# A fused attention and mixture-of-experts block on one core: another order of the opening's loads and products, and another order of products in the expert stage

## The chip, the cores and the metric

The kernel runs on one core of one Trainium2 chip. A core has five engines with queues of their own: TensorE (PE, with its weight loads shown apart as PEld), VectorE (DVE), ScalarE (ACT), GpSimd (POOL) and SyncE (SP). They meet through semaphores. SP, ACT and POOL also issue DMA transfers. The metric is the device time of one execution in microseconds, here the median of the runs. Matmul is meant by "product" below.

## The reference, cut to what matters

x is (2, 256, 32, 32): two images b, 256 channels, 1024 positions ("tokens").

```
h   = group_norm(x, 32 groups) * norm_w + norm_b
q,k,v = conv1x1(h) with wq, wk, wv (+ bq, bk, bv)
x   = x + conv1x1(softmax(q^T k / 16) applied to v, wp) + bp
t   = tokens(x)                                # (2, 1024, 256)
t   = t + autocorrelation_attention(layer_norm(t))   # FFT correlation, top 13 delays, Wq Wk Wv Wo
s   = layer_norm(t) @ Wg + bg                  # 8 experts, top 2, softmax gates
t   = t + sum over the 2 chosen experts e of gate_e * (gelu(ln(t) @ W1[e] + b1[e]) @ W2[e] + b2[e])
```

The expert layer has 256 inputs, 384 hidden units and 256 outputs. Each of the 2048 tokens goes to two experts, so 4096 rows are computed.

## The kernel before, in words

Every engine's queue is a program written out by hand; the order of the work is the order of the statements, and the waits are semaphores with constant values. Most products of 32-bit quality are made as three products of float16 parts (high by high, high by low, low by high); `product` (line 1334) issues them. Others are plain float32 products, which the trace records as two matmul instructions each.

**The opening.** Image 0 must be normalised (h32, then its float16 parts h[0]), and the weights must be combined: A = wq^T wk (line 1379), UW = wv^T wp^T (line 1657, wpT being wp turned, line 1372), and some small vectors ("small", lines 1388 to 1392) of the weights with the biases. The statistics of a channel come from DVE (`channel_stats`, lines 744 and 746), are averaged over a group by a product with a block diagonal matrix (`group_means`, line 1350), then DVE makes the spread (`group_mean`, lines 754 to 758), a second product averages it (`group_spreads`, line 1355), DVE adds eps (line 765), POOL takes the power -0.5 (line 479), and `group_affine` (lines 768 to 770) gives scale and shift. ACT applies them (`normalise`, line 564, one instruction for each half k of the channels). DVE casts to the high part (line 780); the low part of k = 0 is subtracted by POOL (line 483), that of k = 1 by DVE (line 785). With h[0] and A the queries G0 are projected (`project_queries`, line 1334), ACT and DVE take them (lines 548 and 734), and the loop over 16 blocks of scores starts.

The loads: SP issues x of image 0 (two transfers of 512 KB, line 401), the constants (identity and block diagonal, line 403), five vectors of 1 KB each laid out one element for each partition (`cols`, line 405), then x of image 1, the Fourier tables and more. ACT issues the eight weight matrices (lines 539 and 542), all four of the convolution on one semaphore w_in, for which PE waits before wpT. POOL issues the broadcast biases bp_all, bo_all, bg_all and three rows (lines 468 to 472).

PE's order in the opening: wait for the constants and the statistics, group_means, wait for all four weights, wpT, group_spreads, A, wait for the five vectors, small, UW, G0.

`keep_busy` (line 1337, product on line 1340) issues n products of 512 columns whose result nobody reads. The kernel uses them in the middle stages, never in the opening.

**The expert stage.** The 4096 rows and their padding make 39 tiles of 128 rows. For tile s: POOL gathers the rows (line 529, an indirect DMA into one of 6 buffers gx); PE turns them (`turn_gathered`, line 1597, two products into psx, two buffers); ACT takes the high part and DVE the low part into xT (lines 699 and 1191, two buffers); PE makes the hidden layer from 18 float16 products of 128 columns (`hidden`, line 1627); ACT applies gelu (line 708, three instructions); PE makes the result from three float32 products of 256 columns (`results`, line 1639, six recorded instructions); DVE adds the bias (line 1198); POOL scatters the rows (line 533). PE's loop interleaves: in step i it turns tile i, then walks through hidden(i-1), and puts one third of results(i-3) after each fourth, tenth and sixteenth product. Register instructions that form the addresses of the next tile's weights stand inside the same loop. Afterwards the scattered rows are read back, combined, turned and stored.

Of the kernel before, what the change touches and what calls it, by code (L numbers as in the profile page):

```python
# [15 lines left out]
P = 128  # L16
# [89 lines left out]
def conv_attn_moe_kernel(nc, g, out):  # L106
# [3 lines left out]
    with ExitStack() as ctx:  # L110
# [60 lines left out]
        NW, NB, BQ, BK, BV = range(5)  # L171
        bp_all = sb("bp_all", [P, C])
# [14 lines left out]
        prob = view(tiles, 0, [2, N], F32)  # L187
        Pt = [view(tiles, 8 + 4 * i, [2, N], F16) for i in range(2)]
# [109 lines left out]
        w_in, aw_in, small_in, late_in, const_in, fwd_in = sem("w_in"), sem("aw_in"), sem("small_in"), sem("late_in"), sem("const_in"), sem("fwd_in")  # L298
# [14 lines left out]
        consts_made = sem("consts_made")  # L313
# [26 lines left out]
        RESULT_LAG = 3  # L340
# [57 lines left out]
        def _(sp):  # L398
            for b in range(B):
                for k in range(CC):  # L400
                    sp.dma_start(x_sb[b][:, k, :], g["x"][b].rearrange("(k p) a b -> k p (a b)", p=P)[k]).then_inc(x_in[b * CC + k], 16)
                if b == 0:
                    sp.dma_start(const[:, :], g["const_f32"]).then_inc(const_in, 16)
                    for n, name in enumerate(["L0_conv_norm_w", "L0_conv_norm_b", "L0_conv_bq", "L0_conv_bk", "L0_conv_bv"]):
                        sp.dma_start(cols[:, n, :], g[name].rearrange("(k p) -> p k", p=P), allow_slow_non_contiguous=True).then_inc(small_in, 16)
# [59 lines left out]
        def _(pool):  # L465
            PL.memset(half_neg[:, :], -0.5).then_inc(consts_made, 1)
            PL.memset(mean_of_all[:, :], 1.0 / C).then_inc(consts_made, 1)
            pool.dma_start(bp_all[:, :], g["L0_conv_bp"].partition_broadcast(P)).then_inc(late_in, 16)
            pool.dma_start(bo_all[:, :], g["L1_attn_bo"].partition_broadcast(P)).then_inc(late_in, 16)
            pool.dma_start(bg_all[:, :], g["L1_ffn_bg"].partition_broadcast(P)).then_inc(late_in, 16)  # L470
            for n, name in enumerate(["bq", "bk", "bv"]):
                pool.dma_start(qkv_row[:, n * C:(n + 1) * C], g[f"L1_attn_{name}"].rearrange("(a n) -> a n", a=1)).then_inc(late_in, 16)
# [10 lines left out]
            PL.tensor_tensor(h[0][1][:, 0, :], h32[:, 0, :], h[0][0][:, 0, :], ALU.subtract).then_inc(h0_low, 1)  # L483

# [38 lines left out]
            for i in range(TILES + 7):  # L523
                if i == 7:
                    pool.wait_ge(idx_ready, 2)
# [4 lines left out]
                s = i - 7  # L530
# [6 lines left out]
        def _(act):  # L537
            for n, name in enumerate(["wq", "wk", "wv", "wp"]):
                act.dma_start(wraw[:, n, :].rearrange("p (k c) -> p k c", k=CC),
                              g[f"L0_conv_{name}"].rearrange("(k p) c -> p k c", p=P)).then_inc(w_in, 16)  # L540
            for n, name in enumerate(["Wq", "Wk", "Wv", "Wo"]):
                act.dma_start(wraw[:, 4 + n, :].rearrange("p (k c) -> p k c", k=CC),
                              g[f"L1_attn_{name}"].rearrange("(k p) c -> p k c", p=P)).then_inc(aw_in, 16)
# [14 lines left out]
            def normalise(b):  # L558
# [3 lines left out]
                for k in range(CC):  # L562
# [1228 lines left out]
```

## Time and profile before

| | |
|---|---|
| median of 3 runs | 421.17 us (420.97 to 422.4) |
| the profiled execution | 422.2 us, of which the span from first to last instruction is 420.4 us |
| PE busy | 376.8 us, 90% |
| DVE, ACT, POOL busy | 266.6, 156.9, 145.8 us |
| expert stage, first turn to last result | 289.1 to about 395.7 us |

A row of the timeline has the start of a group of like instructions, its length, the engine, the line, and in brackets how long the engine sat idle before it and what ended the wait. A row of the chain of waits is one piece of the path that ended last. The clock column (PEclk) is 1.00 for 2.4 GHz and 0.50 for 1.2 GHz. A matmul's own duration includes its way through the array, so the spacing of back to back products is what counts for a stretch.

### The profile page before, as it was taken

The page shows a single profiled execution, that of the slowest core. Times are in us where ns is not written, and L with a number is a line of the kernel's source. Part 1 is how long each engine was busy: PE and PEld are TensorE (multiplying, and loading weights), DVE is VectorE, ACT ScalarE, POOL GpSimd, SP SyncE. Part 2 cuts the span into 40 slices and gives each one's busy share as a digit, 9 for nine tenths or more (in the row PEclk, how much of TensorE's full clock was granted, in tenths as well). Part 3 has the DMA queues.
Part 4 walks back from the last instruction along what each step waited for, and adds up shares of the span by engine and source line. Part 5 has one row for each costly group of instructions (what it writes and reads, how often), then busy time and mean ns, then how long its engine had stood idle before and what let it go on. Part 6 is the DMA issues. An engine that isn't in the chain of part 4 may idle for free.

```text
span 420.4 us, 7602 instructions
## 1 busy us (share of the span) xinstructions
PE 376.8 (90%) x2651; PEld 263.5 (63%) x2651; DVE 266.6 (63%) x659; ACT 156.9 (37%) x380; POOL 145.8 (35%) x142
## 2 busy tenths in 40 slices
PE   0899999999999989999989999587999999999605
PEld 0745667567666666565566558345888888888505
DVE  3457767568998658989778968984323333233275
ACT  1223476435345325556510000622344444444104
POOL 3202355423424223304100001106677777774400
PEclk9999999999999999999996999979999999999956
DMA  8930000000000007302280002222333233322296
GB/s 229 378 134 2 1 2 2 0 2 1 2 1 2 2 1 173 111 2 75 76 284 5 0 2 80 101 100 67 99 101 99 93 100 102 98 96 74 74 334 255
DMA packets 23077, 35.28 MB, mean 84 GB/s; under 512 B 7296, under 2 KB 16384, under 8 KB 22656
## 3 DMA queue, kind: packets, MB, share of 16 engines
q1 hardware_dynamic: 16896, 22.20, 15.7%
q0 software_dynamic: 3968, 10.50, 8.3%
q10 hardware_dynamic: 2176, 2.10, 1.5%
q8 instruction: 22, 0.36, 0.4%
q14 instruction: 15, 0.12, 0.1%
HBM read 25.48 MB, written 9.31 MB: 83 GB/s over the span
## 4 chain that ended last, share of the span: by engine, by line
PE 73%; DVE 16%; DMA 5%; issue 2%; ACT 1%; POOL 1%; ACTq 0%; SPq 0%; DVEq 0%; POOLq 0%
PE ps L1334 24%; PE ps L1639 13%; PE ps L1627 9%; PE ps L1442 8%; PE ps L1536 3%; PE ps L1340 3%; DMA late<-in_L_conv_wp_dram 2%; PE ps L1597 2%; PE ps L1549 2%; PE ps L1762 1%; DMA tiles<-expert_rows_dram 1%; DVE top_of L821 1%; DVE work L860 1%; DVE t L1206 1%; PE ps L1379 1%
## 5 line engine op out<-in xcount | busy, mean ns | idle before, releaser
L1639 PE MATMUL ps<-l,late 128*128 x234 | 75.0, 406 | 0.0
L500 POOL TENSOR_TENSOR tiles<-tiles 128x512 f16<-128x512 f32 x32 | 38.4, 1221 | 87.7 <-ACT tiles L658 75.7
L1627 PE MATMUL ps<-late,l 128*128 128x128 f16 x702 | 63.5, 219 | 0.3 <-DVE late L1191 0.3
L1627 PEld LDWEIGHTS ps<-late,l 128*128 x702 | 51.6, 98 | 17.1 <-DVE late L1191 0.7
L708 ACT ACTIVATE late<-ps,b_sb 128x128 f32<-128x128 f32 x117 | 34.7, 366 | 58.0 <-PE ps L1627 57.9
L529 POOL DMA_INDIRECT late<-token_rows_dram,idx x39 | 37.9, 971 | 26.8 <-DVE idx L1162 15.2
L1442 PE MATMUL ps<-u_h,tiles 128*128 128x256 f16 x256 | 44.6, 273 | 2.7 <-DVE u_l L835 2.7
L533 POOL DMA_INDIRECT expert_rows_dram<-late,idx x39 | 38.4, 986 | 23.6 <-DVE late L1198 23.0
L1334 PE MATMUL ps<-l 128*128 128x512 f16 x192 | 44.2, 380 | 0.0
L1198 DVE TENSOR_TENSOR late<-ps,qk 128x256 f32<-128x256 f32 x39 | 16.6, 425 | 40.1 <-PE ps L1639 40.1
L1191 DVE TENSOR_TENSOR late<-ps,late 128x256 f16<-128x256 f32 x39 | 16.6, 425 | 34.4 <-ACT late L699 34.4
L1639 PEld LDWEIGHTS ps<-l,late 128*128 128x128 f32 x234 | 35.7, 191 | 0.3
L1442 PE MATMUL ps<-u_l,tiles 128*128 128x256 f16 x128 | 34.9, 272 | 0.0
L652 ACT ACTIVATE tiles<-ps,sm 128x512 f32<-128x512 f32 x32 | 21.7, 684 | 34.4 <-DVE sm L825 34.4
L488 POOL TENSOR_TENSOR trs<-trs,half_neg 128x8 f32<-128x8 f32 (+1 forms) x5 | 6.9, 1384 | 72.2 <-DVE trs L869 64.0
L1334 PEld LDWEIGHTS ps<-l 128*128 128x128 f16 x192 | 17.9, 98 | 22.2 <-issue 2.1
L1334 PE MATMUL ps<-qkvW_h,work 128*128 128x512 f16 (+1 forms) x128 | 30.5, 326 | 0.0
L1442 PEld LDWEIGHTS ps<-u_h,tiles 128*128 128x128 f16 x256 | 25.2, 98 | 6.7 <-DVE u_l L835 3.7
L821 DVE TENSOR_REDUCE top_of<-ps 128x1 f32<-128x512 f32 x32 | 21.5, 688 | 9.5 <-PE ps L1334 7.9
L1340 PE MATMUL ps<-qkvW_h 128*128 128x512 f16 x83 | 23.7, 446 | 0.0
L1334 PE MATMUL ps<-qkvW_l,work 128*128 128x512 f16 (+1 forms) x64 | 20.8, 326 | 0.0
L699 ACT ACTIVATE late<-ps 128x256 f16<-128x256 f32 x39 | 15.3, 392 | 14.9 <-PE ps L1597 14.9
(289 smaller groups left out, 670.2 us busy)
## 6 DMA issues: line engine op xcount, KB each, us to landing
l<-in_L_ffn_W_dram SPq DMA_DIRECT2D x8, 384.0 KB, 6.5
prep<-in_L_ffn_W_dram SPq DMA_DIRECT2D x6, 384.0 KB, 3.5
l<-in_x_dram SPq DMA_DIRECT2D x4, 512.0 KB, 8.0
token_rows_dram<-val SPq DMA_DIRECT2D x2, 1024.0 KB, 3.8
tiles<-expert_rows_dram SPq DMA_DIRECT2D x8, 256.0 KB, 5.0
work<-expert_rows_dram SPq DMA_DIRECT2D x8, 256.0 KB, 6.4
inv_sb<-in_inv_f_dram SPq DMA_DIRECT2D x1, 1536.0 KB, 15.3
out_dram<-l SPq DMA_DIRECT2D x3, 512.0 KB, 2.8
```

The lines of the kernel that those rows point to most:

```text
L500: PL.tensor_tensor(Pt[1][:, n % 2, s], prob[:, n % 2, s], Pt[0][:, n % 2, s], ALU.subtract).then_inc(p_low, 1)
L529: pool.indirect_dma_start(gx[:, i % 6, :], None, xrows, bass.IndirectOffsetOnAxis(idx[:, 0, i:i + 1], 0)).then_inc(gathered[i % 6], 16)
L533: pool.indirect_dma_start(yrows, bass.IndirectOffsetOnAxis(idx[:, 1, s:s + 1], 0), ysb[:, s % 4, :], None).then_inc(scattered[s % 4], 16)
L652: ACTV(prob[:, n % 2, s], psS[:, s], ACT.Exp, bias=sm[:, 2, n:n + 1], accum_out=part[:, half, n:n + 1]).then_inc(s_exp, 1)
L708: last = ACTV(hf[:, s % 3, m * P:(m + 1) * P], psh[s % 2][:, m * P:(m + 1) * P], ACT.Gelu, bias=b1_sb[:, bass.ds(expert, 1), m])
L821: last = V.reduce_max(top_of[:, half, n:n + 1], psS[:, half * HALF:(half + 1) * HALF], AX_X)
L1191: V.tensor_tensor(xT[:, s % 2, 1, :], psx[s % 2], xT[:, s % 2, 0, :], ALU.subtract).then_inc(x_taken, 1)
L1334: last = PE.matmul(dst, lhs, rhs, start=(n == 0), stop=(n == len(seq) - 1))
L1340: PE.matmul(dst, qkvW[0][:, 0, 0:P], qkvW[0][:, 0, 0:512], start=True, stop=True)
L1442: last = PE.matmul(psV[:, j, :], Pt[l][:, n % 2, j * P:(j + 1) * P], u[r][:, n % 2, :], start=False, stop=(i == NT - 1), skip_group_check= ...
L1627: last = PE.matmul(psh[s % 2][:, m * P:(m + 1) * P], weight_in(s, l, k, m), xT[:, s % 2, r, k * P:(k + 1) * P], start=(n == 0), stop=(n == ...
L1639: last = PE.matmul(psy[s % 2], hf[:, s % 3, m * P:(m + 1) * P], weight_out(s, m), start=(m == 0), stop=(m == HC - 1))
```

## The change

In the opening: the constants are loaded first; the five vectors are loaded by POOL as five rows (`col_rows`) and turned by PE into the bank of the group means, from where DVE copies them; POOL's broadcast biases come after its part of h[0]; ACT loads wp, wq, wk, wv, each on a semaphore of its own; SP loads x of image 1 only when these have landed, and then the four attention weights. PE first issues 24 filler products on zeros that DVE has written; group_spreads moves ahead of wpT. ACT takes the high part of A between the two halves of `normalise(0)`, DVE the low part between its two.

In the expert stage: in step i PE turns tile i, issues all of results(i-4), then all of hidden(i-2). psx and xT have three buffers. POOL scatters tile i-8 in its step i, instead of i-7.

```diff
+        COLS_AT = 8
+        col_rows = view(tiles, 0, [C], F32)[0:5, :]
-        for args in [("gn0", 1, "V"), ("wpT", 1, "V"), ("gn0", 1, "V"), ("A", 1, "V", 1), ("small", 1, "V"),
+        for args in [("gn0", 2, "V"), ("wpT", 1, "V"), ("A", 1, "V", 1), ("small", 1, "V"),
-        RESULT_LAG = 3
+        HIDDEN_LAG, RESULT_LAG = 2, 4
-        xT = view(late, 11, [2, 2, CC * P], F16)
+        xT = view(late, 11, [3, 2, CC * P], F16)
-        psx = [ps[:, 0, 0:CC * P], ps[:, 1, 0:CC * P]]
+        psx = [ps[:, n, 0:CC * P] for n in (0, 1, 6)]
 sync
+            sp.dma_start(const[:, :], g["const_f32"]).then_inc(const_in, 16)
             for b in range(B):
+                if b:
+                    for n in range(4):
+                        sp.wait_ge(w_in[n], 16)
                 for k in range(CC):
                     sp.dma_start(x_sb[b][:, k, :], ...)
-                if b == 0:
-                    sp.dma_start(const[:, :], g["const_f32"]).then_inc(const_in, 16)
-                    for n, name in enumerate([... five vectors ...]):
-                        sp.dma_start(cols[:, n, :], g[name].rearrange("(k p) -> p k", p=P), ...).then_inc(small_in, 16)
+            for n, name in enumerate(["Wq", "Wk", "Wv", "Wo"]):
+                sp.dma_start(wraw[:, 4 + n, :]..., g[f"L1_attn_{name}"]...).then_inc(aw_in, 16)
 gpsimd
+            for n, name in enumerate(["norm_w", "norm_b", "bq", "bk", "bv"]):
+                pool.dma_start(col_rows[n:n + 1, :], g[f"L0_conv_{name}"].rearrange("(a n) -> a n", a=1)).then_inc(small_in, 16)
 (wait for consts_made, group_root(0), the low part of h[0] k = 0 now stand here, ahead of the loads of
  bp_all, bo_all, bg_all and the three rows)
-            for i in range(TILES + 7):
-                if i == 7:
+            for i in range(TILES + 8):
+                if i == 8:
                     pool.wait_ge(idx_ready, 2)
-                s = i - 7
+                s = i - 8
 scalar
-            for n, name in enumerate(["wq", "wk", "wv", "wp"]):
+            for n, name in ((WP, "wp"), (WQ, "wq"), (WK, "wk"), (WV, "wv")):
                 act.dma_start(wraw[:, n, :]..., g[f"L0_conv_{name}"]...).then_inc(w_in[n], 16)
-            (the four attention weights)
-            normalise(0)
+            normalise(0, range(1))
             f = FIRST["A"]
             make_high(f, A[0]..., bank(f), scale=ATT_SCALE)
+            normalise(0, range(1, 2))
-            for i in range(TILES + 1):
+            for i in range(TILES + HIDDEN_LAG):
                 if i < TILES:
                     act.wait_ge(x_turned, i + 1)
-                    if i >= 2:
-                        act.wait_ge(hid_full, i - 1)
-                    ACTV(xT[:, i % 2, 0, :], psx[i % 2], ACT.Identity).then_inc(x_high_made, 1)
-                s = i - 1
+                    if i >= 3:
+                        act.wait_ge(hid_full, i - 2)
+                    ACTV(xT[:, i % 3, 0, :], psx[i % 3], ACT.Identity).then_inc(x_high_made, 1)
+                s = i - HIDDEN_LAG
 vector
+            V.memset(qkvW[0][:, 0, 0:512], 0.0).then_inc(zeros_made, 1)
 (group_mean)
+                if b == 0:
+                    V.tensor_copy(cols[:, :, :].rearrange("p n k -> p k n"), bank(f)[:, COLS_AT:COLS_AT + 5 * CC]...)
 (the addition of eps leaves group_affine and is now group_spread, called ahead of the copy of wpT)
-            for k in range(CC):
-                dve.wait_ge(h32_ready, k + 1)
-                (high part k; for k = 1 its low part)
+            dve.wait_ge(h32_ready, 1)
+            V.tensor_copy(h[0][0][:, 0, :], h32[:, 0, :]).then_inc(h0_high, 1)
             f = FIRST["A"]
             low(f, A[1]..., bank(f), A[0]..., scalar=ATT_SCALE)
+            dve.wait_ge(h32_ready, 2)
+            step(V.tensor_copy(h[0][0][:, 1, :], h32[:, 1, :]))
+            V.tensor_tensor(h[0][1][:, 1, :], h32[:, 1, :], h[0][0][:, 1, :], ALU.subtract).then_inc(h0_low, 1)
 tensor
 (group_means)
+                if b == 0:
+                    pe.wait_ge(small_in, 16 * 5)
+                    for k in range(CC):
+                        PE.transpose(dst[:, COLS_AT + 5 * k:COLS_AT + 5 * (k + 1)], col_rows[:, k * P:(k + 1) * P], ident[0:5, 0:5])
                 pe.wait_ge(mean_ready, b + 1)
+            pe.wait_ge(zeros_made, 1)
+            keep_busy(ps[:, 7, :], 24)
             pe.wait_ge(const_in, 16)
             group_means(0)
-            pe.wait_ge(w_in, 64)
+            group_spreads(0)
+            pe.wait_ge(w_in[WP], 16)
             (wpT)
-            group_spreads(0)
+            pe.wait_ge(w_in[WQ], 16)
+            pe.wait_ge(w_in[WK], 16)
             (A)
-            pe.wait_ge(small_in, 16 * 5)
+            wait_taken(pe, FIRST["gn0"])
             (small)
+            pe.wait_ge(w_in[WV], 16)
             (UW)
 (turn_gathered)
-                if s >= 2:
-                    pe.wait_ge(x_taken, s - 1)
+                if s >= 3:
+                    pe.wait_ge(x_taken, s - 2)
 (the loop of the expert stage)
-                first = hidden(i - 1) if 0 <= i - 1 < TILES else iter(())
-                second = results(i - RESULT_LAG) if 0 <= i - RESULT_LAG < TILES else iter(())
+                if 0 <= i - RESULT_LAG < TILES:
+                    results(i - RESULT_LAG)
+                first = hidden(i - HIDDEN_LAG) if 0 <= i - HIDDEN_LAG < TILES else iter(())
                 for n in range(3 * HC):
                     next(first, None)
                     next(first, None)
-                    if n % 3 == 1:
-                        next(second, None)
-                    if n == 4 and i < TILES:
-                        hidden_addresses(i)
+                    if n == 4 and 0 <= i + 1 - HIDDEN_LAG < TILES:
+                        hidden_addresses(i + 1 - HIDDEN_LAG)
```

## Rows read from the trace of the kernel before

**Rows 1.** The page: the clock in 40 slices, and the chain by engine.
```profile
PEclk9999999999999999999996999979999999999956
...
PE 73%; DVE 16%; DMA 5%; issue 2%; ACT 1%; POOL 1%; ACTq 0%; SPq 0%; DVEq 0%; POOLq 0%
```

**Rows 2.** Chain of waits, opening: start us, length us, what.
```profile
14.07 3.62 PE ps L1379 x8
17.69 3.20 PE ps L1388 x16
...
22.79 3.38 PE ps L1657 x8
26.17 1.31 PE ps L1334 x6
```

**Rows 3.** Lines 1379 and 1657 (A, UW): duration ns min/median/max, first to last start.
```profile
L1379 PE MATMUL ps<-late x8: 634/634/774, 13.9 to 17.1; 128*128 128x256 f32 x8
...
L1657 PE MATMUL ps<-prep,late x8: 380/634/796, 22.7 to 25.8; 128*128 128x256 f32 x8
```

**Rows 4.** Timeline of the opening: start us, length us, engine, line.
```profile
7.06 1.29 DVE L744 BATCH_NORM_STATS2 bn<-l 128x6 f32<-128x512 f32 x2 [0.61 <-DMA l<-in_x_dram]
8.38 0.21 DVE L746 BATCH_NORM_AGGREGATE mv<-bn 128x2 f32<-128x12 f32 x1
...
11.23 0.58 PE L1350 MATMUL ps<-mv,const 128*128 128x2 f32 x2 [11.23 <-DMA const<-in_const_f_dram]
...
12.44 0.16 DVE L758 TENSOR_TENSOR gn<-gn,mv 128x2 f32<-128x2 f32 x1
...
13.64 0.43 PE L1355 MATMUL ps<-gn,const 128*128 128x2 f32 x2
...
14.49 0.15 DVE L765 TENSOR_SCALAR gn<-ps 128x2 f32<-128x2 f32 x1
...
18.37 2.13 POOL L483 TENSOR_TENSOR l<-work,l 128x1024 f16<-128x1024 f32 x1 [2.85 <-DVE l L780]
...
18.73 2.32 DVE L780 CAST l<-work 128x1024 f16<-128x1024 f32 x1 [0.44 <-ACT work L564]
...
21.08 1.23 DVE L785 TENSOR_TENSOR l<-work,l 128x1024 f16<-128x1024 f32 x1
```

**Rows 5.** Chain of waits, one tile of the expert stage.
```profile
318.29 0.49 PE ps L1639 x2
318.78 0.34 PE ps L1627 x6
...
320.54 0.23 PE ps L1597 x2
```

**Rows 6.** Chain of waits from 205 us: six fillers.
```profile
220.30 2.67 PE ps L1340 x6
```

**Rows 7.** Windows: stretch, its length, PE busy, clock, DMA share, GB/s.
```profile
224.00:225.00 1.00, 1.00 (x36) 1.00 0.07 16
```

**Rows 8.** Line 1639 from 393 us on, where its products follow one another.
```profile
L1639 PE MATMUL ps<-l,late x12: 379/379/435, 392.9 to 395.3; 128*128 x12
```

**Rows 9.** Chain of waits, a gather's transfer where the expert stage begins.
```profile
287.43 2.79 DMA late<-token_rows_dram,idx
```

**Rows 10.** Timeline, where the expert stage begins.
```profile
288.71 0.95 POOL L529 DMA_INDIRECT late<-token_rows_dram,idx  x1 [0.30 <-issue]
...
290.66 1.18 PE L1627 MATMUL ps<-late,l 128*128 128x128 f16 x18
```

**Rows 11.** POOL's groups from 300 to 390 us: busy us, mean ns, idle before.
```profile
L533 POOL DMA_INDIRECT expert_rows_dram<-late,idx x34 | 33.6, 987 | 18.4 <-DVE late L1198 17.8 <-issue 0.6
L529 POOL DMA_INDIRECT late<-token_rows_dram,idx x30 | 29.1, 971 | 9.1 <-issue 9.1
```

**Rows 12.** DMA issues up to 24 us: KB each, median us to landing.
```profile
late<-in_L_attn_bq_dram POOLq DMA_DIRECT2D x1, 1.0 KB, 6.9
```

**Rows 13.** Waits from 24 to 190 us: us in total, times, longest.
```profile
PEld ps L1334 <- issue: 10.3, 37, 1.0
```

More of the change, by code:

```diff
@@ L297, in conv_attn_moe_kernel @@
         x_in = [sem(f"x_in{q}") for q in range(B * CC)]
-        w_in, aw_in, small_in, late_in, const_in, fwd_in = sem("w_in"), sem("aw_in"), sem("small_in"), sem("late_in"), sem("const_in"), sem("fwd_in")
+        w_in = [sem(f"w_in{n}") for n in range(4)]
+        aw_in, small_in, late_in, const_in, fwd_in = sem("aw_in"), sem("small_in"), sem("late_in"), sem("const_in"), sem("fwd_in")
         inv32_in = sem("inv32_in")
@@ L483, in _ @@
             PL.tensor_tensor(h[0][1][:, 0, :], h32[:, 0, :], h[0][0][:, 0, :], ALU.subtract).then_inc(h0_low, 1)
+            pool.dma_start(bp_all[:, :], g["L0_conv_bp"].partition_broadcast(P)).then_inc(late_in, 16)
+            pool.dma_start(bo_all[:, :], g["L1_attn_bo"].partition_broadcast(P)).then_inc(late_in, 16)
+            pool.dma_start(bg_all[:, :], g["L1_ffn_bg"].partition_broadcast(P)).then_inc(late_in, 16)
+            for n, name in enumerate(["bq", "bk", "bv"]):
+                pool.dma_start(qkv_row[:, n * C:(n + 1) * C], g[f"L1_attn_{name}"].rearrange("(a n) -> a n", a=1)).then_inc(late_in, 16)
             def rstd(n, b, js=slice(0, NT)):
@@ L537, in _ @@
         def _(act):
-            for n, name in enumerate(["wq", "wk", "wv", "wp"]):
+            for n, name in ((WP, "wp"), (WQ, "wq"), (WK, "wk"), (WV, "wv")):
                 act.dma_start(wraw[:, n, :].rearrange("p (k c) -> p k c", k=CC),
[L540 to L543, printed above, removed]
+                              g[f"L0_conv_{name}"].rearrange("(k p) c -> p k c", p=P)).then_inc(w_in[n], 16)
             def make_high(f, dst, src, **kw):
@@ L556, in attn_weight_high, with normalise @@
                 make_high(f, qkvW[0][:, :, w * C:(w + 1) * C], bank(f).rearrange("p (k c) -> p k c", k=CC))
-            def normalise(b):
+            def normalise(b, ks=range(CC)):
                 act.wait_ge(affine_ready, b + 1)
@@ L561, in normalise @@
                     act.wait_ge(h0_low, CC)
-                for k in range(CC):
+                for k in ks:
                     q = b * CC + k
@@ L758, in group_mean, with group_spread @@
                 V.tensor_tensor(gn[:, 4, q], gn[:, 4, q], mv[:, q, 1], ALU.add).then_inc(spread_ready, 1)
+            def group_spread(b):
+                f = fills(f"gn{b}")[1]
+                full(f)
+                V.tensor_scalar(gn[:, 5, b * CC:(b + 1) * CC], bank(f)[:, 0:CC], EPS_CONV, None, ALU.add).then_inc(v_taken, 1)
             def group_affine(b):
                 q = slice(b * CC, (b + 1) * CC)
-                f = fills(f"gn{b}")[1]
-                full(f)
-                V.tensor_scalar(gn[:, 5, q], bank(f)[:, 0:CC], EPS_CONV, None, ALU.add).then_inc(v_taken, 1)
-                dve.wait_ge(small_in, 16 * 5)
                 dve.wait_ge(root_ready, b + 1)
@@ L1593, in turn_gathered @@
                 pe.wait_ge(gathered[s % 6], 16 * (s // 6 + 1))
-                if s >= 2:
-                    pe.wait_ge(x_taken, s - 1)
+                if s >= 3:
+                    pe.wait_ge(x_taken, s - 2)
                 for k in range(CC):
-                    last = PE.transpose(psx[s % 2][:, k * P:(k + 1) * P], gx[:, s % 6, k * P:(k + 1) * P], ident)
+                    last = PE.transpose(psx[s % 3][:, k * P:(k + 1) * P], gx[:, s % 6, k * P:(k + 1) * P], ident)
                 last.then_inc(x_turned, 1)
@@ L1626, in hidden @@
                     for n, (l, r, k) in enumerate([(l, r, k) for k in range(CC) for l, r in ((0, 0), (0, 1), (1, 0))]):
[L1627 removed]
+                        last = PE.matmul(psh[s % 2][:, m * P:(m + 1) * P], weight_in(s, l, k, m), xT[:, s % 3, r, k * P:(k + 1) * P],
                                          start=(n == 0), stop=(n == 3 * CC - 1))
@@ L1639, in results @@
                     last = PE.matmul(psy[s % 2], hf[:, s % 3, m * P:(m + 1) * P], weight_out(s, m), start=(m == 0), stop=(m == HC - 1))
-                    if m == HC - 1:
-                        last.then_inc(y_full, 1)
-                    yield
+                last.then_inc(y_full, 1)
             at_expert = [None] * 16
@@ L1750, in _ @@
                 for _ in first:
-                    pass
-                for _ in second:
                     pass
```

27 lines of the change are left out of this document (9 added, 18 removed).

## The prediction

> **What bounds the kernel now.** I read the chain by engine first, then the opening and the expert stage in the chain of waits and the timeline. PE holds 73% of the chain [rows 1]: what shortens PE's own work or lets it begin earlier counts, the rest mostly doesn't.
>
> The opening: the chain runs through the weights' products, A, small, UW and then the first half of G0, with no wait between them from 12.7 us on [rows 2]. The reader is to see how slow they are. A's eight products take 3.62 us, 0.45 each, and each lasts 634 ns; UW's last one lasts only 380 [rows 3]. The clock column shows full speed in the first slices [rows 1], but the same kind of product can't last 634 and 380 ns at one clock: up to about 25.7 us PE ran at the lower of its two levels (1.2 GHz), and the column merely has no record there. Ahead of PE stand the loads: the statistics were ready at 8.59 us, but the means' product began at 11.23, when the constants had landed, and the spreads' product waited behind wpT until 13.64, though DVE was done at 12.60 [rows 4].
>
> The expert stage: PE without a gap. A tile is three pairs of L1639 at 0.49 us, 18 products of L1627 at 0.056 and the turn, 0.23 [rows 5]: 1.46 + 1.00 + 0.23 = 2.69 us; 39 of them are the stretch from 289 to 396 us.
>
> **Part 1, the opening.** Loads: the constants (128 rows of 328 floats, 0.17 MB) now stand ahead of x on SP's queue. That queue moved x's two halves, 1 MB, within the first 7.06 us [rows 4], at least 0.15 MB/us, so x comes at most 1.1 us later; the element-wise vectors and broadcasts that ran beside it are gone. Bounds: 0 and 1.1 us; I take 0.6. With 1.53 us from landing to statistics (7.06 to 8.59), they are ready at 7.66 + 1.53 = 9.2 us. The turned vectors (four short products) lie before that, in PE's waiting time.
>
> The fillers: 24 products from about 1.3 us on, behind DVE's memset. At the lower clock one took 2.67 / 6 = 0.445 us [rows 6], at the higher 1.31 / 6 = 0.218 [rows 2]. All fast, they end at 6.5 us; all slow, at 12.0. In the middle of the kernel six slow fillers from 220.3 us on and what followed them had the clock back at 1.00 in the window 224:225 [rows 7]. With 8 to 15 slow ones, they end between 8.4 and 10.0; I take 9.2. So the means' product begins at 9.3 instead of 11.23.
>
> From there by the rows: 1.37 us to DVE's end (11.23 to 12.60), and 0.2 for the copy of the vectors now ahead of it: the spreads' product at 10.9. DVE adds eps 0.48 later, at 11.4, since it no longer has wpT's copy in front. From that instruction to the last part of h[0] it was 14.49 to 21.08 + 1.23 = 22.31, 7.8 us [rows 4]: now 19.2. ACT's high part of A, put between the halves of `normalise`, costs the second half 0.6 us, but nothing here: in before the second cast took 2.32 us, because it waited for POOL's subtraction that ran from 18.37 to 20.50 [rows 4], and it will again. Without that cover it would be 0.6 us.
>
> PE beside it: wpT at 11.0, then at the higher clock A 8 x 0.22 = 1.8, the 16 short ones of small 3.20 / 2 = 1.6, the rest of small about 1.2, UW 3.38 / 2 + 0.3 = 2.0 [rows 2], with wpT's 0.5 together 7.1: done at 18.1, before h[0]. G0 thus begins at 19.25 where it began at 26.0 [rows 3, 2]: **6.8 us gained**. What is late next is h[0], by 1.1 us. DVE's own row (small 1.5 us, UW's low part 0.7) ends at 21.4, as ACT has G0's first half: no further delay. From G0 on the steps are the same and no load ends a wait: image 1 is first read at 37 us and would land by some 13, the attention weights are turned at 55 us, POOL's six late issues (3.5 us) end ten microseconds before its next work. These I cost at nothing; were x of image 1 late, its statistics would hold DVE's softmax one to one.
>
> The Trainium skill, SBUF — State Buffer, "Who interferes with whom", has this as a rule: one instruction gets the port pair that DVE and GpSimd share, and the other fully blocks. The cast's 2.32 us agree. By the same page GpSimd can't write its descriptors while DVE holds the pair, which speaks against loads on POOL's queue; this is the rival "late rows" below.
>
> **Part 2, the expert stage.** The first product of each pair of L1639 lasts 435 ns, the second 379. Where twelve follow one another, the median is 379 and only the first has 435 [rows 8]: the 0.056 us are paid where a float32 product follows a float16 one, and its weights are loaded behind a product of 56 ns. Before: three such places in a tile. Now the row of six stands behind the turn (0.115 us each), and pays none. So 3 x 0.056 = 0.168 us for each of the 37 tiles whose results were interleaved: 6.2 us. Bounds: 4.1 us if the first of the row still pays, 6.2 if none does; I take the second, since the turn's products are longer than the extra time.
>
> The start costs. A gather is landed 2.8 us after its issue [rows 9]; the third is issued at 288.71 [rows 10], so landed at 291.5, and hidden(0), at 290.66 before [rows 10], now waits behind it: 291.8. With the fourth and fifth gathers 1.25 us apart, and results(0) behind the fifth turn, the work done at 296.6 us is 0.4 us behind the old order. The end is the same: two rows of results without anything beside them.
>
> Would another engine bind at 2.69 - 0.17 = 2.52 us? POOL needs 0.99 + 0.97 and twice 0.30 us between [rows 11]: 2.57. That is 0.05 a tile more, 1.7 us over 34 tiles; by the code a gather stands behind the scatter of a tile nine back, which is ready some four steps before the gathered tile is turned; less the issues on POOL and 2.8 us to land, some 6 us are spare, so I cost it at nothing (1.7 us if the spare isn't there). ACT and DVE are idle half of the stage. Hence **5.8 us gained**.
>
> **Sum.** 6.8 + 5.8 = 12.6 us. The profiled execution takes 422.2 us (span 420.4 and 1.8 around it), 1.0 over the median of the runs: 409.6 for such a one, 408.6 for the median.
>
> **Rivals.**
> (a) The clock is not up for A. Then PE's work from A on lasts as before, 26.0 - 13.9 = 12.1 us; with wpT slow (1.1) A starts at 11.9, G0 at 24.0: 2.0 us instead of 6.8, in all 413.4. For it: after the fillers PE has only short or two-column products until A. Against: fillers of this length brought the level back in mid-kernel [rows 7], and 1.1 us of slack absorbs a part. The Trainium skill, TensorE: Matmul & The Clock Gate, "Part 4: PE-mode transpose", says transposes don't count as busy; by it wpT and the vectors wouldn't hold the clock. No row separates this.
> (b) Late rows. The fifth row would be issued at 3.7 us; the POOL-issued row of before landed 6.9 us after its issue [rows 12], which makes 10.6 and delays the means, now behind `small_in`, by 1.3: 409.9. Against: those loads ran beside broadcasts of 128 KB.
> (c) The stage doesn't speed up: POOL's queue or the gathers bind, or the 0.056 stay. Then 421.2 - 6.8 + 0.4 = 414.8. Against it stand the twelve in a row [rows 8].
> (d) Slower: the address registers. After the row of six come 18 products in a run, and the register instructions stand among them. In the softmax stage PE's loads stalled for issue 37 times, 10.3 us, 0.28 each [rows 13]. Twice per tile that is 39 x 0.56 = 21.8 us: 421.2 - 12.6 + 21.8 = 430.4. It decides from 1.15 stalls a tile on. Against: at 290.66 us 18 products ran in 1.18 us [rows 10], with such instructions among them.
> (e) Faster still: x as early as before, fillers done by 8.4, and a stretch at the lower clock between 220 and 231 us that falls elsewhere: 2 to 3 us more, 406.
>
> **Chances.** Forecast 55% (its own range, with the clock's drift in the middle stages: 406.8 to 410.6), b 10% (within that range), a 16%, e 8%, c 7%, d 2%, a and c together (419) 2%. The range 405.0 to 414.0 leaves out d, the last, and parts of c and e. About 0.3% (1.3 us) is what a measurement tells from no change: faster 0.96, same 0.02, slower 0.02.
>
> **What would show it.** The fillers' spacing falls from 0.43 to 0.216 us within the first 9 us, and A's products last 380 ns. The means' product starts at 9 to 10 us, G0 at 19 to 20 behind h[0]'s last part on DVE. The tile's period is 2.52 us, with L1639's median at 379 ns and at most one of 435 a tile; 2.57 with PE waiting for gathers means POOL binds. Wrong: products of 634 ns at 12 us (a), a wait of PE for the rows' loads (b), a stall for issue in the run of 18 (d), or a new DMA wait after 30 us.

## The result, and the profile after

The changed kernel takes 414.64 us (median of four runs, 412.95 to 415.29) against 421.07 us (419.38 to 422.4) for the kernel before on the same chip: ratio 0.9844, 95% interval 0.9804 to 0.9884. It is faster by 6.4 us (1.6%), about half of the 12.6 forecast, and 414.64 lies above the range's upper end of 414.0. Ratios and their intervals, here and below, leave out executions that took over 1.5% longer than the fastest of their kernel; medians and ranges have all of them.

The page of the changed kernel, clock and chain, answers to [rows 1].
```profile
PEclk9899999999999999999986999969899999999958
...
PE 75%; DVE 14%; DMA 5%; issue 2%; SPq 1%; POOL 1%; ACT 1%; DVEq 0%; ACTq 0%; POOLq 0%
```
Its opening, in the timeline (start us, length us, engine, line), answers to [rows 4].
```profile
4.80 3.19 PE L1351 MATMUL ps<-qkvW_h 128*128 128x512 f16 x14
...
8.27 1.28 DVE L752 BATCH_NORM_STATS2 bn<-l 128x6 f32<-128x512 f32 x2 [0.86 <-DMA l<-in_x_dram]
8.95 0.25 PE L1365 MATMUL ps<-const,tiles 5*128 5x5 f32 x2 [0.97 <-DMA tiles<-in_L_conv_bv_dram]
9.59 0.21 DVE L754 BATCH_NORM_AGGREGATE mv<-bn 128x2 f32<-128x12 f32 x1
9.85 0.38 PE L1367 MATMUL ps<-mv,const 128*128 128x2 f32 x2 [0.65 <-DVE mv L754]
...
11.77 0.16 DVE L774 TENSOR_SCALAR gn<-ps 128x2 f32<-128x2 f32 x1 [0.68 <-PE ps L1372]
...
12.48 2.83 PE L1400 MATMUL ps<-late 128*128 128x256 f32 x8
12.73 0.69 DVE L789 COPY prep<-ps 128x512 f32<-128x512 f32 x1 [0.80 <-PE ps L1392]
...
13.34 0.15 DVE L780 TENSOR_TENSOR gn<-gn,cols 128x2 f32<-128x2 f32 x1
...
18.68 1.22 DVE L797 TENSOR_TENSOR l<-work,l 128x1024 f16<-128x1024 f32 x1
...
19.96 2.76 PE L1345 MATMUL ps<-l,prep 128*128 128x512 f16 x12
...
22.34 0.75 DVE L741 SCALAR_TENSOR_TENSOR l<-ps,gq,l 128x512 f16<-128x512 f32 x1 [0.38 <-ACT l L554]
```
The fillers end near 8.0, the turned vectors wait for their rows until 8.95, and the means' product follows the statistics at 9.85. DVE's copy of wpT (line 789) stands between the addition of eps (line 774) and the scale (line 780). G0 starts at 19.96, when h[0]'s last part ends (18.68 + 1.22); predicted was 19.25.

A's products (line 1400) show the clock in their durations, as [rows 3] did.
```profile
L1400 PE MATMUL ps<-late x8: 379/558/634, 12.5 to 14.9; 128*128 128x256 f32 x8
```
The first are slow, the last fast: the clock was granted from 4.15 us on, fell to 0.50 at 10.97 and rose again at 14.39.

The expert stage's start in the chain of waits, beside [rows 10].
```profile
286.45 0.44 PE ps L1618 x2
286.89 1.28 PE ps L1648 x18
288.17 0.43 PE ps L1618 x2
288.60 1.92 PE ps L1648 x18
290.52 0.43 PE ps L1618 x2
290.94 1.32 PE ps L1660 x6
292.26 1.00 PE ps L1648 x18
293.27 0.23 PE ps L1618 x2
```
The run of 18 hidden products takes 1.00 us at the full clock, but 1.92 at 288.60, and a turn 0.43 instead of 0.23. The windows (stretch and length; busy PE, PEld, DVE, ACT, POOL; clock, DMA share, GB/s) say why:
```profile
287.50:290.80 3.30, 3.30 (x30) 3.23 (x28) 0.69 (x2) 1.31 (x5) 2.65 (x3) 0.50 0.38 118
...
296.00:380.00 84.00, 84.00 (x862) 75.75 (x861) 28.01 (x66) 38.96 (x135) 61.43 (x63) 1.00 0.32 100
```
From 293 us on the stage runs as forecast: line 1660's median is 379 ns, and turns follow at 2.53 us where they did at 2.69.
```profile
L1660 PE MATMUL ps<-l,late x203: 379/379/435, 295.9 to 379.9; 128*128 x102
```
The waits from 296 to 380 us (us in total, times, longest) hold no row of PE. POOL's gaps for issue of 0.3 us stood mostly ahead of the gathers in [rows 11]; now they stand in both lines. POOL is nearly full (61.4 us busy and 16.1 us in such gaps, of 84), and PE doesn't wait for it.
```profile
POOL expert_rows_dram L542 <- issue: 9.4, 31, 0.3
POOL late L538 <- issue: 6.7, 22, 0.3
```

### The profile page after: what moved, and what is told of

It is laid out like the page before. It is cut to its first block, busy times and chain, and to the rows that moved or that the text cites. A ratio compares the mean times of both kernels' runs of the same rounds, so it can differ in the third digit from the quotient of the medians.

```text
span 411.0 us, 7655 instructions
## 1 busy us (share of the span) xinstructions
PE 376.4 (92%) x2677; PEld 265.6 (65%) x2677; DVE 266.0 (65%) x661; ACT 157.0 (38%) x380; POOL 148.7 (36%) x147
## 4 chain that ended last, share of the span: by engine, by line
PE 75%; DVE 14%; DMA 5%; issue 2%; SPq 1%; POOL 1%; ACT 1%; DVEq 0%; ACTq 0%; POOLq 0%
PE ps L1345 25%; PE ps L1660 12%; PE ps L1648 10%; PE ps L1463 8%; PE ps L1557 3%; PE ps L1351 3%; PE ps L1618 2%; PE ps L1550 2%; PE ps L1570 2%; DMA tiles<-expert_rows_dram 2%; DMA l<-in_x_dram 2%; PE ps L1780 2%; DVE top_of L831 1%; DVE work L870 1%; PE ps L1590 1%
## 5 line engine op out<-in xcount | busy, mean ns | idle before, releaser
L1660 PE MATMUL ps<-l,late 128*128 x234 | 57.0, 380 | 0.0
L538 POOL DMA_INDIRECT late<-token_rows_dram,idx x39 | 37.9, 972 | 27.2 <-DVE idx L1172 15.6
L1648 PEld LDWEIGHTS ps<-late,l 128*128 x702 | 43.6, 99 | 5.4
L1648 PE MATMUL ps<-late,l 128*128 128x128 f16 x702 | 46.8, 222 | 0.0
L1660 PEld LDWEIGHTS ps<-l,late 128*128 128x128 f32 x234 | 41.6, 191 | 4.1
L1351 PE MATMUL ps<-qkvW_h 128*128 128x512 f16 x107 | 31.8, 461 | 1.2 <-DVE qkvW_h L743 1.2
L1208 DVE TENSOR_TENSOR late<-ps,qk 128x256 f32<-128x256 f32 x39 | 16.6, 424 | 20.9 <-issue 14.1
L1463 PEld LDWEIGHTS ps<-u_h,tiles 128*128 128x128 f16 x256 | 25.2, 98 | 6.8 <-DVE u_l L845 3.7
L1351 PEld LDWEIGHTS ps<-qkvW_h 128*128 128x128 f16 x107 | 12.1, 118 | 16.9 <-issue 8.5
```

The costliest lines, as they stand in the source:

```text
L538: pool.indirect_dma_start(gx[:, i % 6, :], None, xrows, bass.IndirectOffsetOnAxis(idx[:, 0, i:i + 1], 0)).then_inc(gathered[i % 6], 16)
L1351: PE.matmul(dst, qkvW[0][:, 0, 0:P], qkvW[0][:, 0, 0:512], start=True, stop=True)
L1463: last = PE.matmul(psV[:, j, :], Pt[l][:, n % 2, j * P:(j + 1) * P], u[r][:, n % 2, :], start=False, stop=(i == NT - 1), skip_group_check= ...
L1648: last = PE.matmul(psh[s % 2][:, m * P:(m + 1) * P], weight_in(s, l, k, m), xT[:, s % 3, r, k * P:(k + 1) * P], start=(n == 0), stop=(n == ...
L1660: last = PE.matmul(psy[s % 2], hf[:, s % 3, m * P:(m + 1) * P], weight_out(s, m), start=(m == 0), stop=(m == HC - 1))
```

## The experiments

Landmarks used below: z, the start of DVE's first low part of the projected queries G0, where the opening ends; the first gather; the start of the last scatter. A turn is PE's turning of one tile's rows. Each set ran on a chip of its own. On four of these chips the kernel before took 442.9 to 445.7 us; on the fifth 420.8, as on the chip where the result was taken (below: the first chip).

### Set 1: the parts

`opening_only` is the changed kernel with the expert stage of before, `stage_only` the kernel before with the new stage, `after_again` the changed kernel, and `no_fillers` leaves out this line:
```diff
-            keep_busy(ps[:, 7, :], 24)
```


> The opening of the changed kernel with the expert stage of before. Theory 1 (each part gives what its stretch of the two profiles shows, 6.0 us up to G0's taking, less what the clock takes in the middle stages): 5 to 6 us faster, ratio 0.986 to 0.988, G0 begins at 20.0 us, the tile stays at 2.69 us. Theory 2 (the middle stages give the gain back, because they end in waits on loads or on the clock): under 3 us faster, and the expert stage begins less than 4 us earlier than before although G0 begins 6 us earlier.

> The opening of before with the expert stage of the changed kernel. Theory 1: tile 2.525 us, 37 tiles give 6.2 us, the start of the stage costs 0.4 us at the full clock and up to 1.7 us more where a stretch at the lower clock falls on it: 4 to 5.8 us faster, ratio 0.986 to 0.990. Theory 2 (POOL's 2.57 us for a tile binds in most executions, or the deeper pipeline costs at the end): 2 us or less. A start without any row of 0.50 in the clock would show 5.8.

> The changed kernel as it is, on one chip with its parts. Theory 1: the sum of the two parts within 1 us, 9 to 11 us faster (ratio 0.974 to 0.979) where the lower clock falls as in the profile, 6.5 where it falls worse; a second profile shows G0 again at 20.0 and the tile at 2.525, and other places for the stretches at 0.50. Theory 2: the parts do not add, the whole is no better than the better part.

> The changed kernel without the 24 filler products at the start. Theory 1 (the fillers bring the clock up before the weights' products): the products of A and UW last 634 ns again, PE's row takes 12 us from A on, G0 begins at about 24 us instead of 20.0, the time is 3.5 to 4.5 us longer than the changed kernel's. Theory 2 (the clock would be up anyway by A, or falls again before it, as it did at 11.0 us in the profile): no more than 1 us longer.

Ratios to before (442.87 us): 0.9935 (0.9901 to 0.9968), 1.0199 (1.0143 to 1.0254), 1.0167 (1.0122 to 1.0212) and 1.0074 (1.0023 to 1.0124). None of my theories had the new stage 2% slower. The profiles say where: up to the stage all is as on the first chip, and in it ACT, DVE and PE stand still for several us at a time. By its ratio the opening alone gains 2.9 us (1.4 to 4.4), not the 5 to 6 that I expected: its z comes at 22.11, but that of `stage_only`, which has the old opening, at 25.51 and not at 28.4. Without fillers z comes at 22.21, with them at 21.25 and 22.11 on this chip and 22.34 on the first: they moved the opening by under 1 us, as theory 2 of `no_fillers` had it. Its times (441.7 to 458.2 us) are too far apart to show more.

### Set 2: is it the chip, the row or the lags?

`before_2` and `after_2` are the two kernels unchanged. `start_fillers` adds to the loop of the stage
```diff
+                if i < 2:
+                    keep_busy(ps[:, 7, :], 3)
```
and `new_lags_mixed` spreads the results between the hidden products again:
```diff
-                if 0 <= i - RESULT_LAG < TILES:
-                    results(i - RESULT_LAG)
...
+                    if n % 3 == 1:
+                        next(second, None)
```


> The kernel before, unchanged, for a second profile of it. Theory 1 (its time on the other chip was 22 us longer because the expert stage alone stalls there for instructions): where this chip is like the first, its profile shows 37 tiles in 2.69 us each with no stop of TensorE on issue and the run takes 419 to 423 us; where it is like the second, the stage up to the last scatter is 20 us longer than in the first profile, everything ahead of it is within 1 us, and TensorE's stops are on issue. Theory 2 (that chip is slower throughout, by its memory or its clock): the 20 us are spread over the opening, the middle stages and the tail by their lengths.

> The changed kernel, unchanged, for a second profile and more times of it. Theory 1 (the executions of it differ by where the granted clock falls to 0.50, in the middle stages and at the start of the expert stage): on a chip like the first, 413 to 416 us, opening 6.0 us shorter than before at the first z (22.3 against 28.4), steady tile 2.52 to 2.53 us, and one clock fall at the start of the stage that costs 1 to 2 us. Rival (instructions come late to TensorE in the stage in some executions of this chip too): pieces of the 18 hidden products 0.7 us apart in its profile, a mean tile above 2.6 us, 416 us or more.

> The changed kernel, with three filler products into a free bank behind each of the first two turns of the expert stage. Theory (at the start of the stage TensorE waits for the first tiles, the clock falls to 0.50 for 3.4 us and costs 1.7 us): the clock stays at 1.00 there, turn 5 comes 7.5 us after turn 0 instead of 9.2, and the run is 1.0 to 1.7 us shorter than the changed kernel beside it. Rival (the start is set by the gathers and ScalarE, and the fall of the clock only fills waits): turn 5 comes 9.0 to 9.4 us after turn 0, the run is within 0.5 us or up to 0.6 us longer, for the fillers' own time.

> The changed kernel with its turns two steps ahead, three buffers and results four steps behind, but the six result products spread between the hidden ones again as in the kernel before, not in one row. Theory 1 (on a chip that supplies TensorE's instructions in time, the row alone gives the stage's gain, since an f32 weight load behind a short fp16 product is exposed by 0.056 us three times a tile): steady tile 2.69 us as before, run 5 to 6 us longer than the changed kernel beside it, so close to the opening's gain alone. Theory 2 (on a chip that supplies them late, the row makes it worse, since 36 of a tile's instructions then fall within 1.0 us): there the mixed order is 4 to 10 us shorter than the changed kernel. Rival (the deeper lags give or cost the time): it runs as the changed kernel does, within 1 us, on either chip.

Times 445.92, 449.62, 453.66 and 439.37 us; ratios to before (445.45 us) 0.9998, 1.0084 (1.0041 to 1.0127), 1.0128 (1.0027 to 1.023) and 0.9896 (0.985 to 0.9942). The stage alone is longer in `before_2`: 134.1 us from the first gather to the last scatter, 110.5 in the first profile; what stands ahead of it takes as long as there. Its timeline shows a stop.
```profile
340.67 0.27 PE L1627 MATMUL ps<-late,l 128*128 128x128 f16 x2
...
341.72 0.50 PE L1627 MATMUL ps<-late,l 128*128 128x128 f16 x6
...
343.21 0.42 DVE L1198 TENSOR_TENSOR late<-ps,qk 128x256 f32<-128x256 f32 x1 [3.44 <-remote]
343.23 0.89 ACT L708 ACTIVATE late<-ps,b_sb 128x128 f32<-128x128 f32 x3 [4.39 <-remote]
```
The hidden products of a tile end at 340.94 (the first row), and ACT should take them at once. It starts 2.3 us later, in the same moment as DVE, while PE works on. The trace's semaphore events have PE's increment for 340.94 at 343.11, and beside it, from 343.06 to 343.15, those for a turn and for a result. So PE did the work in time and its signals arrived late, several together; theory 1 had the place right, but these stops aren't on issue. Counted so (over 0.3 us late, last hidden product of a tile; a few records are missing, so the counts are rough): none of 39 in the two first profiles, 20 in `before_2`, 23 in `after_2`, 16 in `new_lags_mixed`, whose profiled execution (447.12 us) was the longest of its five. In `after_2` the clock fell to 0.50 five times between 290 us and the last scatter, in `after` not once. Mixed results were 10 us shorter than the row here: the row is worse under late increments, by what detail isn't shown. `start_fillers` says nothing under this noise: its turn 5 came 15.6 us after turn 0, far beyond both 7.5 and 9.2.

### Set 3: what makes the increments late?

```diff
 # fixed_weights
-                at = at_expert[s % 16] * EXPERT_BYTES + 2 * (l * CC * H + k * H + m * P)
+                at = (s % E) * EXPERT_BYTES + 2 * (l * CC * H + k * H + m * P)
 # wide_products
-                        last = PE.matmul(psh[s % 2][:, m * P:(m + 1) * P], weight_in(s, l, k, m), ...
+                        last = PE.matmul(psh[s % 2], weight_in(s, 0, k, m), ... [:, 0:3 * P], ...
 # half_transfers, i >= 12
-                    pool.indirect_dma_start(gx[:, i % 6, :], None, xrows, ...
+                        PL.memset(idle[:, i:i + 1], 0.0).then_inc(gathered_2, 1)
```
`fixed_weights` leaves out the choice of a tile's expert, `wide_products` the low part of the hidden weights, and `half_transfers` the gathers from tile 12 on. `x_first` moves the load of the constants behind the two halves of image 0.

> The changed kernel, but each tile of the expert stage takes the weights of a fixed expert, so TensorE reads no addresses from registers (it leaves out the choice of the tile's expert on TensorE); the count of its products is the same. On the chips of the two earlier sets TensorE's semaphore increments came 1 to 5 us late in about 20 of 39 tiles. Theory 1 (the addresses held in registers make TensorE late): 0 to 2 late tiles, steady tile 2.53 us throughout, last scatter some 25 us earlier, run 0.93 to 0.95 of the kernel before. Theory 2 (what counts is how many instructions TensorE must be given a us, 26 loads and 26 products in 2.53 us): about as many late tiles as in the changed kernel, ratio 0.99 to 1.02. Theory 3 (POOL's indirect transfers disturb it): the same as theory 2.

> The changed kernel with the 18 hidden products of 128 columns replaced by six of 384 columns (it computes something else: the weights' low part is left out); TensorE's columns and their time stay, its weight loads and products go from 52 to 28 a tile, and its register addresses from 24 to 12. Theory 1 (registers) and theory 2 (instructions a us): both expect 0 to 4 late tiles and a tile near 2.5 us, ratio 0.93 to 0.96; with the fixed weights beside it they are told apart. Theory 3 (POOL's indirect transfers): late tiles as before, about half of them, ratio 0.99 to 1.02.

> The changed kernel, but from tile 12 on no rows are gathered (a 1-element memset on POOL signals in their place, so stale rows are used); the scatters stay. Theory 3 (POOL's indirect transfers disturb TensorE's signals): late tiles after tile 12 fall to half or less, ratio 0.95 to 0.98. Theories 1 and 2: about half the tiles are late as before, ratio 0.99 to 1.02.

> The changed kernel with the two halves of the first image loaded ahead of the constants. Theory (the opening's missing 0.6 to 0.7 us is the second half of x, which landed at 8.25 us instead of the predicted 7.66): the second half lands at 7.4 to 7.7, statistics end at 9.1 to 9.3, the first z product starts 0.5 to 0.7 us earlier than in the changed kernel (22.3). Rival (all transfers of the opening share the engines, and the constants are then late for the means product instead): the half lands 0.3 us sooner at most, or the means product waits for the constants, and z is within 0.2 us. The run's time on such a chip is set by the late tiles, 1.00 to 1.02 of before, either way.

With before at 445.67 us: `fixed_weights` took 451.45 (ratio 1.0027 to 1.0184) and has 21 late tiles, so it is not the registers. `wide_products` took 437.11 (0.9692 to 0.9856), still with 22 late: halving PE's instructions gains 2% and doesn't remove them. `half_transfers` took 419.7 (0.9313 to 0.9479) and has five late tiles, the last at 309 us, where the gathers end; every turn after that comes 2.53 us behind the last. Theory 3 holds. The waits from 320 to 380 us of `half_transfers` have four rows and nothing "remote"; those of `after_2` from 296 to 405 had
```profile
ACT late L715 <- remote: 34.4, 6, 7.1
...
PEld ps L1648 <- issue: 11.2, 19, 1.3
```
`x_first` took 449.05 us. Its second half landed at 6.40, 1.4 us before that of `after_again` (7.82), whose clock stayed up in the opening too; but the means' product still began at 9.11, behind the fillers and the turned vectors, and z came at 20.93, only 0.3 us before that of `after_again` (21.25). The gain is nearly as small as the rival had it, by another wait than it named.

### Set 4: the stages without late increments

These kernels leave out the gathers from tile 6 on, or replace them.

```diff
 # quiet_new_stage, quiet_old_stage, quiet_fillers: i >= 6
-                    pool.indirect_dma_start(gx[:, i % 6, :], None, xrows, ...
+                        PL.memset(idle[:, i:i + 1], 0.0).then_inc(gathered_2, 1)
 # plain_loads: i >= 6, on SP
+                sp.wait_ge(x_turned, i - 5)
+                sp.dma_start(gx[:, i % 6, :], xrows[(i % TT) * P:(i % TT + 1) * P, :])...
```


> The changed kernel, with rows gathered for the first six tiles alone (from the seventh on a small memset on POOL signals in their place and stale rows are used). Theory (with the gathers gone, TensorE's increments are in time and the stage goes as in the first profile): no late tile after tile 8, steady tile 2.53 us. It is the base for the two kernels beside it.

> The same without gathers from the seventh tile on, the changed kernel's opening, but the expert stage's order of before (turn one step ahead with two buffers, results three steps behind and spread between the hidden products). Theory (the row saves 0.168 us a tile and the start costs 0.4 us more): steady tile 2.69 us, run 5.5 to 6.5 us longer than the quiet new stage. Rival (the start of the new order gives back what the row saves): 3 to 4.5 us longer, with the start of the new stage 1.5 us or more longer by the profiles and the clock at 0.50 in it.

> The quiet new stage with three filler products behind each of the first two turns. Theory (the fall of the clock at the start of the stage costs 1 to 2 us): the clock stays at 1.00 through the first three hidden tiles and the run is 1.0 to 1.7 us shorter than the quiet new stage. Rival (the start is set by the gathers, or the clock falls later instead): within 0.5 us of it, or longer.

> The changed kernel with the rows of tile 6 on brought by plain transfers on SP's queue (the same 128 KB a tile, in the order of the rows, not of the tokens), not gathered by POOL; POOL's scatters stay. Theory A (what makes TensorE's increments late is POOL's gathers as indirect transfers): no late tiles after the first eight or so, time of the quiet new stage within 1.5 us. Theory B (it is the traffic into SBUF, or that of reading and writing HBM at once): late tiles as with the gathers, 440 us or more, 20 us above the quiet new stage.

Here before took 444.75 us, the four 415.02, 421.67, 414.4 and 412.6 (ratios 0.9315, 0.948, 0.9303, 0.9283, each within 0.006). `plain_loads` moves the same bytes and has PE late only at the stage's start, while six tiles are gathered. That is theory A: it is the gathers as POOL's indirect transfers, not the bytes that they bring. (The plain transfers also read their rows in order; gathers on a POOL without scatters weren't tried, so it may take both.) Steady tiles are 2.53 and 2.69 us. The old stage is 6.65 us longer than the new, just above the 5.5 to 6.5 that I gave, but not for that reason alone: in its profile 4.3 us are late increments at its start, while the six gathers run (turn 5 came 14.0 us after turn 0; 9.7 in [rows 10]'s execution). `quiet_fillers` is 0.6 us from its base, within the noise; in its profile the clock fell at 282.2, ahead of the first turn. So fillers there showed no gain; whether they would where the clock falls behind them, this doesn't show.

### Set 5: both kernels, on a chip like the first

The same edit (no gathers from tile 6 on) on the kernel before and on the changed one.

> The kernel before, without gathers from the seventh tile on (stale rows are used; a small memset on POOL signals in their place). Theory 1 (the profile that the prediction rests on shows a rare opening; the usual one has its clock at 1.00 from 16 to 18 us on): first z low part at 25.0 to 25.6, steady tile 2.69 us, and a time of 423 to 426 us, 8 to 11 us above quiet_after, of which 3 to 4 us are the opening's and the rest the stage's, with late increments in its start counted in. Rival (the clock rises near 25.7 as a rule, and the two other profiles were the exceptions): z at 28.0 to 28.6, 427 us or more, 12 to 13 us above quiet_after as predicted.

> The changed kernel in the same form, as in quiet_new_stage, for the same chip as quiet_before. Theory 1: 413 to 416 us, first z low part at 21 to 22.4, turn 5 of the stage 9.0 to 9.3 us after turn 0, ratio of the two quiet kernels 0.974 to 0.981. Rival: the same time, ratio 0.968 to 0.972. What remains between 8 to 11 us here and 6.5 us on the first chip would be the late increments in the start of the old stage, which the first chip does not have.

This time the chip was of the first kind: before 420.77 us (418.18 to 426.2, 17 runs). `quiet_before` takes 421.18 (ratio 0.9998, 0.9964 to 1.0033) where I gave 423 to 426. So the gathers cost nothing there, and its profile has no late tile. `quiet_after` takes 413.44 (409.06 to 414.7; ratio 0.9815, 0.976 to 0.987), 7.7 us less, below the 8 to 11 that I gave. The opening of `quiet_before`, for [rows 2, 3]:
```profile
13.57 3.76 PE L1384 MATMUL ps<-late 128*128 128x256 f32 x8
17.12 2.15 PE L1393 MATMUL ps<-cols,late 128*128 128x1 f32 x16
...
20.26 1.99 PE L1665 MATMUL ps<-prep,late 128*128 128x256 f32 x8
22.80 2.75 PE L1339 MATMUL ps<-l,prep 128*128 128x512 f16 x12 [0.55 <-DVE prep L739]
```
A is slow as in [rows 2], but UW takes 1.99 us, not 3.38, and G0 begins at 22.80, behind DVE, not at 26.0 behind PE. What it waits for is DVE's low part of A, which stands behind h[0]'s last part. In the execution that I predicted from, that was done at 22.91, and PE wasn't:
```profile
22.22 0.69 DVE L734 SCALAR_TENSOR_TENSOR prep<-ps,prep 128x512 f16<-128x512 f32 x1
```
The clock rose at 17.8 us in `quiet_before`, at 16.5 in `before_2`, at 17.5 in `stage_only`, and at 25.7 only in that first execution; why so late there isn't shown. In `quiet_after` the clock stays up at the stage's start:
```profile
285.21 1.17 PE L1656 MATMUL ps<-late,l 128*128 128x128 f16 x18
...
286.45 1.17 PE L1656 MATMUL ps<-late,l 128*128 128x128 f16 x18
...
287.72 1.46 PE L1668 MATMUL ps<-l,late 128*128 x6
...
289.01 1.17 PE L1656 MATMUL ps<-late,l 128*128 128x128 f16 x18
```
Turn 5 comes 7.3 us after turn 0, where `after` needed 9.2. It isn't the missing gathers: `quiet_new_stage`, the same kernel on another chip, needed 9.2 as well, with the clock at 0.50 from 289.4 us on, 3.2 us behind its first turn.

## Why the prediction was wrong

By stretch, in us, from the four profiles of chips of the first kind:

| | before | after | change | quiet_before | quiet_after | change |
|---|---|---|---|---|---|---|
| to z | 28.4 | 22.3 | -6.0 | 25.2 | 22.4 | -2.7 |
| z to first gather | 257.6 | 258.5 | +0.9 | 259.4 | 256.9 | -2.5 |
| to last scatter | 110.5 | 106.5 | -4.0 | 110.5 | 105.0 | -5.5 |
| to the end | 23.8 | 23.6 | -0.3 | 24.5 | 23.3 | -1.1 |

- **The sum, the step that failed.** "409.6 for such a one, 408.6 for the median" carried a gain reckoned against one execution over to the median. Of the opening's term of 6.8 us, some 3.2 belonged to that execution's late clock (z at 28.4; 25.2, 25.2 and 25.5 in the three other profiles of the old opening). With the clock up from 16.5 to 17.8 us on, G0 was bound by DVE (h[0], then the low part of A) and not by PE, and began at 22.8 to 23.2 instead of 26.0. Against that the new opening gains 2.7 to 2.9 us. The prediction saw that PE ran at 1.2 GHz until 25.7 us, and took it for the rule; its own trace had DVE done at 22.91, which would have made the term 3.7.
- **The opening's mechanism** was right in its order: statistics, means, spreads, h[0], then G0. x landed 0.6 us later than taken (8.25 for 7.66). The steps up to eps won back 0.2 of that, but DVE's copy of wpT, now between eps and the scale, cost 0.3: 1.57 us from line 774 to 780, where the same step took 1.24 before. G0 came 0.7 later than forecast. Rival (b) fell: the rows had landed by 8.95. Rival (a) came in part: after the fillers, PE had only the short products of the vectors, means and spreads, and the clock fell before A in `after`. In 15 profiles with the fillers it stayed at 1.00 through the rest of the opening in six, was down for 3.4 us in seven, and for 10.2 us in two, whose z came at 25.2 and 25.5 (20.9 to 22.5 in the others). The Trainium skill, TensorE: Matmul & The Clock Gate, "Part 4: PE-mode transpose", says that transposes don't count as busy in the same way as other products. No run here shows or refutes it, since PE also stood idle beside them (1.0 us before the turned vectors, 0.65 behind them).
- **The fillers** brought the clock early and the time hardly: `no_fillers` has its clock up from 14.3 us on and z at 22.21. Since h[0] is the limit, A's speed is worth little; the opening's gain is mostly that of loads and order.
- **The stage** was right where the clock held: 0.166 us a tile (2.693 to 2.527) for the 0.168 forecast, no stall for issue, POOL without cost, and 5.5 us in the quiet pair (`quiet_before` and `quiet_after`) where 5.8 was forecast. In `after` the start took 1.9 us more than in `quiet_after`, when the clock was at 0.50 from 287.45 to 290.87. I had charged the start for gathers alone (0.4), and the stage's term of 5.8 us measured 4.0 there.
- **The middle** isn't touched, and yet z to the first gather ran from 256.9 to 261.6 us over all profiles, with 12 to 28 us at 0.50 in it. Rival (e) counted such a stretch as luck on one side; it is the spread of every run. `quiet_after` took 409.1 to 409.7 us with a mean clock of 0.962 to 0.965, and 413.1 to 414.7 with 0.945 to 0.954: 408.6 is near what the change gives with the highest mean clock seen, not its median.

Put together from other profiles: 2.8 us in the opening and 4.0 to 5.5 in the stage are 6.8 to 8.3; measured are 6.4 on the first chip (4.9 to 8.3) and 7.7 in the quiet pair. The size of each part in the median isn't measured closer than that. The times of two rivals, 413.4 of (a) and 414.8 of (c), lie near the measured one by accident: G0 began at 20.0 and not at 24.0, and the tile did become 0.166 us shorter. Rival (d) named the right danger, PE starved in the row, with the wrong cause; its 21.8 us are close to what the other chips show, but those show it in the kernel before as well.

## What to carry to other kernels

Before a gain at a clock-limited stretch is priced, ask what the stretch costs in another execution of the same kernel: where the product durations show a late clock, compute the sum a second time with the clock up and see what binds then. A filler is worth only what the next limit leaves. And a stage that is tuned to 2.5 us a tile with POOL's gathers beside it should be timed on several chips: the order that wins on one (results in a row) lost 2% on others, where the spread order, with the new opening and the deeper lags, won 1%.

## What the hardware showed

- On four of the experiments' five chips the kernel before takes 22 to 25 us longer and the changed one about 35, all of it in the expert stage: with POOL gathering rows and scattering them, PE's increments reach the other engines late in about half the tiles, mostly by 1 to 6 us. With scatters alone, or the same bytes on SP's queue, they do not; the changed kernel's 450 us became 413 to 420. On the fifth chip the gathers cost nothing (ratio 0.9998). What differs between the chips, and why gathers and not scatters, is open. Gathers of fewer bytes, and gathers without scatters, weren't tried.
- The clock column has no record before the first change: "1.00" in the first slices of before covered products at half speed, up to 25.7 us. The products' durations show it (634 ns for 380).
